# Graph message layer on one core: three changes ahead of the periods (first receivers, x's differences, inverse lengths)

## The reference

```
r = edge_vec / norm(edge_vec);  sh1 = sqrt(3) * r
xs, xd = x[src], x[dst]                       # sender's and receiver's rows
w  = relu(emb @ w1 / sqrt(10)) @ w2 / sqrt(16)    # per-edge weights, 512 and 384 of them
s_t, v_t  = products of (xs, xd) with w and sh1   # first layer
scal, gates, vecs = products of (s_t, v_t) with w2 and sh1
edge_out = [tanh(scal), vecs * tanh(gates)] * edge_weight
out = layernorm(x + segment_sum(edge_out, dst))
```

## Time and profile before

| | us |
|---|---|
| median of 3 runs | 6613.86 |
| these runs | 6610.04 to 6614.21 |
| profiled execution, its own time | 6605.81 |
| span of that execution | 6604.0 |
| first DMA of the first period's loads issued at | 62.45 |
| first product of the periods on VectorE (L1233) starts at | 105.46 |

### The profile page before, as it was taken

How to read it: one execution, slowest core, us unless ns; L and a number is a source line. 1 busy time by engine, 2 the same in 40 slices (tenths; PEclk the granted TensorE clock), 3 DMA queues, 4 the chain that set the end, 5 groups by cost and what they waited for, 6 DMA issues and landing times.

```text
span 6604.0 us, 217789 instructions
## 1 busy us (share of the span) xinstructions
PE 5916.6 (90%) x67802; PEld 5648.0 (86%) x67802; DVE 5987.5 (91%) x7727; ACT 4058.7 (61%) x12100; POOL 5021.9 (76%) x6871
## 2 busy tenths in 40 slices
PE   2999999999999999999999999999989999999997
PEld 2888888888888888888888888888888888888887
DVE  6999999999999999999999999999999999999998
ACT  3666666666666666666666666666666666666664
POOL 4777777777777777777777777777777777777774
PEclk9999999999999999999999999999999999999998
DMA  4444444444444444444444444444444444444442
GB/s 126 86 89 84 86 87 85 85 87 86 84 86 88 84 87 86 84 86 88 84 86 88 84 86 88 84 88 86 86 89 84 86 88 84 88 86 86 87 85 54
DMA packets 1671528, 569.93 MB, mean 86 GB/s; under 512 B 1535556, under 2 KB 1619493, under 8 KB 1670946
## 3 DMA queue, kind: packets, MB, share of 16 engines
q1 hardware_dynamic: 1568321, 516.43, 35.3%
q0 software_dynamic: 103168, 53.03, 6.0%
HBM read 302.19 MB, written 7.26 MB: 47 GB/s over the span
## 4 chain that ended last, share of the span: by engine, by line
PE 75%; issue 13%; DVE 5%; ACT 3%; another core or an unknown queue 3%; DVEq 1%; ACTq 0%; DMA 0%; POOL 0%; SPq 0%; POOLq 0%
PE p L982 42%; PE pw L977 18%; PE p L1068 4%; PE ph L965 2%; PE ph L954 2%; PE p L1061 2%; PE p L1063 1%; PE p L1029 1%; PE p L1011 1%; DVE prods L1275 1%; ACT hot_t L741 1%; PE p L1012 1%; DVEq L1434 1%; ACT osum L820 0%
## 5 line engine op out<-in xcount | busy, mean ns | idle before, releaser
L982 PE MATMUL p<-identity,prods 128*128 128x128 f32 x29016 | 3642.6, 279 | 7.8 <-issue 6.7
L647 POOL DMA_INDIRECT nodes<-x_rows,idx x3224 | 3114.5, 966 | 603.7 <-issue 515.9
L982 PEld LDWEIGHTS p<-identity,prods 128*128 128x128 f32 x29016 | 3292.0, 146 | 36.5 <-issue 12.3
L977 PE MATMUL pw<-w_stack,hid_t 128*128 128x128 bf16 x22568 | 1702.4, 223 | 116.2 <-issue 52.4
L977 PEld LDWEIGHTS pw<-w_stack,hid_t 128*128 128x128 bf16 x22568 | 1433.6, 100 | 216.7 <-issue 98.2
L1275 DVE TENSOR_TENSOR prods<-pw,M 128x1024 f32<-128x1024 f32 x806 | 977.1, 1212 | 38.5 <-PE pw L977 24.8
L1233 DVE TENSOR_TENSOR prods<-pw,V 128x2048 f32<-128x2048 f32 x403 | 914.4, 2269 | 9.4 <-ACT acc L926 6.3
L1252 DVE TENSOR_TENSOR prods<-pw,S 128x1024 f32<-128x1024 f32 x403 | 491.8, 1220 | 327.6 <-remote 190.7
L838 ACT ACTIVATE off_hot<-node_iota,off_base 128x42 f32<-128x42 f32 x3216 | 752.6, 317 | 13.0
L1285 DVE TENSOR_TENSOR prods<-pw,VT 128x1536 f32<-128x1536 f32 x403 | 705.2, 1750 | 23.9 <-PE pw L977 19.4
L594 POOL TENSOR_TENSOR msg<-th,late 128x128 f32<-128x128 f32 x403 | 164.0, 407 | 728.7 <-ACT th L819 390.8
(11 more groups left out here) (130 smaller groups left out, 8205.5 us busy)
## 6 DMA issues: line engine op xcount, KB each, us to landing
dstb<-in_dst SPq DMA_DIRECT2D x403, 504.0 KB
nodes<-x_rows,idx POOLq DMA_INDIRECT x3224
emb_stack<-emb_parts SPq DMA_DIRECT2D x2418, 20.0 KB
emb<-in_emb_t SPq DMA_DIRECT2D x403, 40.0 KB
hid_t<-hid_parts SPq DMA_TRANSPOSE x806
idx<-in_src SPq DMA_DIRECT2D x403, 4.0 KB
xw<-x SPq DMA_DIRECT2D x403, 7.9 KB
vecs<-in_vec SPq DMA_DIRECT2D x403, 12.0 KB
```

Of the source, the lines that this page charges most:

```text
L647: nc.gpsimd.indirect_dma_start(nodes[:, p, t, side, :], None, x_rows, bass.IndirectOffsetOnAxis(ap=idx[:, p, side, t:t + 1], axis=0)).then ...
L977: mm = nc.tensor.matmul(pw[:, slot, t, :], hid_t[:, layer, a.par, t, :], w2_stack[:, lo:lo + W], start=True, stop=True)
L982: return nc.tensor.matmul(out, column, identity[:, :], start=first, stop=last, is_transpose=True)
```

## The change

Three things, all ahead of the periods. `base_i` is no longer loaded. TensorE waits for `s_excess` and turns the four columns of `span[:, 2, :]` into one row with four small matmuls, into `p1`; VectorE copies the row (and the last super's number) into `base_i`. The four subtractions of x's pieces go from VectorE to GpSimd, in its list between `emb_less_second` of super 0 and `partition_all_reduce`, for which it now also waits until all eight steps of `x_cast` are done; `x_parted` is gone. Squares, sums, roots and reciprocals of the lengths are made in three parts each (1088, 1088 and 1056 of 3232 per partition), and roots and reciprocals move from the body of i = -1 to ahead of the program: ScalarE's roots ahead of its reading of the flag, VectorE's reciprocals behind its own.

```
@@ SyncE
-            sp.dma_start(base_i[0:1, 0:FULL], dst[0:FULL * SUPER].rearrange("(a s e) -> a s e", a=1, e=SUPER)[:, :, 0],
-                         allow_slow_non_contiguous=True).then_inc(s_base_in, 16)
-            if NS != FULL:
-                sp.dma_start(base_i[0:1, FULL:NS], dst[E - SUPER:E - SUPER + 1].rearrange("(a s) -> a s", a=1)
-                             ).then_inc(s_base_in, 16)
...
-                sp.wait_ge(s_inv, 1)
+                sp.wait_ge(s_inv, len(thirds))
...
-            sp.wait_ge(x_parted, 1)
+            sp.wait_ge(x_cast, 8)
             sp.dma_start(x3.rearrange("(p b) a f -> p (b a f)", p=P),
@@ GpSimd
             emb_less_second(At(0, 0))
+            for h in range(2):
+                half = xn[:, h * (NB // 2):(h + 1) * (NB // 2), :]
+                parts = x_parts[:, h * (NB // 2):(h + 1) * (NB // 2), :, :]
+                pool.wait_ge(x_cast, 4 * h + 1)
+                nc.gpsimd.tensor_tensor(x_rest, half, parts[:, :, 0, :], ALU.subtract).then_inc(x_cast, 1)
+                pool.wait_ge(x_cast, 4 * h + 3)
+                nc.gpsimd.tensor_tensor(parts[:, :, 2, :], x_rest, parts[:, :, 1, :], ALU.subtract).then_inc(x_cast, 1)
+            pool.wait_ge(x_cast, 8)
             pool.wait_ge(s_excess, 1)
             nc.gpsimd.partition_all_reduce(excess_all[:, :], excess_one[:, :], P, RMAX).then_inc(s_excess_all, 1)
@@ ScalarE
                 act.wait_ge(x_in, 16 * len(x_pieces))
+                wait(act, x_cast, 4 * h)
                 nc.scalar.activation(parts[:, :, 0, :], half, ACT.Copy).then_inc(x_cast, 1)
...
-            nc.scalar.activation(all_vectors, all_vectors, ACT.Square).then_inc(s_squared, 1)
+            for lo, hi in thirds:
+                nc.scalar.activation(all_vectors[:, 3 * lo:3 * hi], all_vectors[:, 3 * lo:3 * hi], ACT.Square
+                                     ).then_inc(s_squared, 1)
+            for g, (lo, hi) in enumerate(thirds):
+                act.wait_ge(s_norm2, g + 1)
+                nc.scalar.activation(inv[:, lo:hi], inv[:, lo:hi], ACT.Sqrt).then_inc(s_length, 1)
             act.wait_ge(row_node_done, 2)
             act.wait_ge(s_general, 1)
...
-                    if i == -1:
-                        act.wait_ge(s_norm2, 1)
-                        nc.scalar.activation(inv[:, :], inv[:, :], ACT.Sqrt).then_inc(s_length, 1)
@@ TensorE
             pe.wait_ge(s_const, 11)
+            pe.wait_ge(s_excess, 1)
+            for c in range(SCAN):
+                mm = nc.tensor.matmul(p1[0:1, P * c:P * c + P], span[:, 2, c:c + 1], identity[:, :], start=True, stop=True)
+            mm.then_inc(s_bases, 1)
             pe.wait_ge(s_general, 1)
@@ VectorE
-            for h in range(2):
...
-                nc.vector.tensor_tensor(x_rest, half, parts[:, :, 0, :], ALU.subtract).then_inc(x_cast, 1)
...
-            dve.sem_inc(x_parted, 1)
...
+            dve.wait_ge(s_bases, 1)
+            nc.vector.tensor_copy(base_i[0:1, 0:FULL], p1[0:1, 0:FULL]).then_inc(s_base_in, 1)
+            if NS != FULL:
+                nc.vector.tensor_copy(base_i[0:1, FULL:NS], span[0:1, 2, SCAN:SCAN + 1]).then_inc(s_base_in, 1)
...
-            dve.wait_ge(s_base_in, 32 if NS != FULL else 16)
+            dve.wait_ge(s_base_in, NS - FULL + 1)
             flag = nc.vector.value_load(general[0:1, 0:1], min_val=0, max_val=1)
...
-            dve.wait_ge(s_squared, 1)
-            nc.vector.tensor_reduce(inv[:, :], all_vectors.rearrange("p (e k) -> p e k", k=3), AX.X, ALU.add
-                                    ).then_inc(s_norm2, 1)
+            for g, (lo, hi) in enumerate(thirds):
+                dve.wait_ge(s_squared, g + 1)
+                nc.vector.tensor_reduce(inv[:, lo:hi], all_vectors[:, 3 * lo:3 * hi].rearrange("p (e k) -> p e k", k=3), AX.X,
+                                        ALU.add).then_inc(s_norm2, 1)
+            for g, (lo, hi) in enumerate(thirds):
+                dve.wait_ge(s_length, g + 1)
+                nc.vector.reciprocal(inv[:, lo:hi], inv[:, lo:hi]).then_inc(s_inv, 1)
...
-                    if i == -1:
-                        dve.wait_ge(s_length, 1)
-                        nc.vector.reciprocal(inv[:, :], inv[:, :]).then_inc(s_inv, 1)
```

More of the change, by code:

```diff
@@ L220, in build_gnn_layer @@
         s_base_in = sem("s_base_in")
+        s_bases = sem("s_bases")
         s_scan_in = sem("s_scan_in")
@@ L223, in build_gnn_layer @@
         x_cast = sem("x_cast")
-        x_parted = sem("x_parted")
         x3_out = sem("x3_out")
@@ L390, in build_gnn_layer @@
         vec_pieces = in_pieces(all_vectors, vec.rearrange("e k -> (e k)"), vec_rows_full, 3 * ER, 0, 3 * ER, 3 * vec_last)
+        third_of = 16 * -(-ER // 48)
+        thirds = [(g * third_of, min(ER, (g + 1) * third_of)) for g in range(3)]
         per_bank = 512 // F
@@ L511, in _ @@
             sp.wait_ge(x3_out, 16)
-            sp.wait_ge(s_base_in, 32 if NS != FULL else 16)
+            sp.wait_ge(s_base_in, NS - FULL + 1)
             sp.wait_ge(s_general, 1)
@@ L923, in body @@
                     if i in (0, 1):
-                        act.wait_ge(s_norm2, 1)
+                        act.wait_ge(s_norm2, 3)
                         lo, hi = (0, ACC // 2) if i == 0 else (ACC // 2, ACC)
@@ L1195, in _ @@
             nc.vector.tensor_reduce(excess_one[:, :], excess[:, :], AX.X, ALU.max).then_inc(s_excess, 1)
-            for h in range(2):
-                half = xn[:, h * (NB // 2):(h + 1) * (NB // 2), :]
-                parts = x_parts[:, h * (NB // 2):(h + 1) * (NB // 2), :, :]
-                dve.wait_ge(x_cast, 4 * h + 1)
-                nc.vector.tensor_tensor(x_rest, half, parts[:, :, 0, :], ALU.subtract).then_inc(x_cast, 1)
-                dve.wait_ge(x_cast, 4 * h + 3)
-                ins = nc.vector.tensor_tensor(parts[:, :, 2, :], x_rest, parts[:, :, 1, :], ALU.subtract)
-                ins.then_inc(x_cast, 1)
-                dve.wait_ge(x_cast, 4 * h + 4)
-            dve.sem_inc(x_parted, 1)
             dve.wait_ge(s_const, 11)
```

## The result

The changed kernel takes 6663.95 us in the median (6654.34 to 6666.22, four runs), the kernel before beside it 6614.03 (6610.04 to 6622.14, four runs): ratio 1.0071, interval 1.0054 to 1.0089. It is 50 us slower where 14.6 us faster was forecast, and the prediction is wrong. The profiled execution has a span of 6664.3 us, 60.3 over that of before.

The account below looks back on a forecast made before the run. With TensorE 90% busy, only the start of the periods was taken to move. Gains of 11.3 us (GpSimd and ScalarE path) and 3.3 us (inverse lengths) made 14.6, so 6613.86 became 6599.3 us, range 6593 to 6610.

Parts of the forecast that it names:

- What bounds the kernel: Whole span: TensorE is busy 90% and a period's work is untouched, so only the start of the periods can move.
- The last sentence of the prediction: Signs of a wrong forecast: all-reduce over 3 us off 47, x3 later than 45, or a period's work changing pace.
- Part 1: Start, SyncE: without base_i's loads x3 is stored at 42, lands at 49.1, and SyncE reaches the first period 12.4 us earlier.
- Part 2: Start, GpSimd: four subtractions at 3.2 us each, from 19.91 to 37.6, so x3's store at 42 does not wait.
- Part 3: Start, behind GpSimd's subtractions: reload 7.7, all-reduce 1.8, sums from 48.3, row_shift at 59.8; gain cut to 11.3 us.
- Part 4: Start, inverse lengths in thirds: their store at 90.2 no longer waits 4.06 us for VectorE; less 0.8, gain 3.3 us.
- The sum: Whole kernel: 11.3 + 3.3 = 14.6 us gained, all at the start, giving 6599.3 us.
- A: Start, SyncE: x_rows's backlog holds whatever stands next, x3 goes at 54.4, only 3.3 us gained, 6610.6; chance 0.12.
- B: Start, GpSimd's path longer: 3.8 to 4.5 us a subtraction or reload over 10, 6601.5 to 6606; chance 0.2.
- C: Start, GpSimd's path shorter (2.6 to 3.0 us, reload 6), SyncE's path decides, gain 12.4 + 3.3 to 4.1, 6597.5; chance 0.17.
- D: Start, GpSimd: subtractions cost 16.5 ns a column, 26 us each, so 77 us lost, 6690; chance 0.03.

Follow-up runs that it names:

- f2: Changed kernel plus two idle semaphore increments on SyncE in place of the two base_i loads, against the kernel before: 6542.06 us beside 6555.18, ratio 0.9979.
- j2: The same kernel as f2, run again against the kernel before: 6543.88 us beside 6553.51, ratio 0.9986.
- h3: f2's kernel plus 32 increments at the start of VectorE's list, against the kernel before: 6023.02 us beside 6037.13, ratio 0.9975.
- e1: Kernel before with only the base_i loads replaced by TensorE's matmuls and VectorE's copies, against the kernel before: 6087.09 us beside 6039.16, ratio 1.0075.
- h1: Kernel before plus 63 idle increments on SyncE ahead of the loop, against the kernel before: 6098.14 us beside 6037.13, ratio 1.0101.
- h2: Kernel before plus 62 idle increments on SyncE ahead of the loop, against the kernel before: 6094.9 us beside 6037.13, ratio 1.0099.
- h4: Kernel before plus four increments on SyncE inside the loop, once per pair of periods, against the kernel before: 6115.19 us beside 6037.13, ratio 1.0132.

## Why the prediction was wrong, step by step

- **What bounds the kernel**: this step failed. "So it can only move the point at which the periods begin to run at their pace" was drawn from TensorE's 90%. SyncE is not in that row, and its waits over the periods were not read. With two instructions fewer ahead of its loop, SyncE takes 0.22 us longer around the back branch of every pair, at an edge of its list. At the higher clock it has no slack (no row of waits), and the pair is 0.31 us longer, 197 times; on the chip of the result it has 7%, and the pair is 0.36 us longer all the same. So the periods lost 73 us where the prediction had nothing, and the start's 13.2 stand against them. That the edit would touch SyncE's pace could not be read from the trace of before; that SyncE has little to spare could. The last sentence of the prediction named this case, and gave it no chance.
- **Part 1**: right. The stacks went out and the last ones were held, to 40.02; x3 at 40.06 for 42. But it landed 10.9 us later and not 7.1, at 50.99 for 49.1. So idx was 10.5 us earlier, not 12.4: this term is 1.9 too large. The copy to x_rows landed only at 43.0 (issued at 12.18, 30.8 us), so x3's store ran beside it for its first 3 us, where before x3 went out 10 us after that landing (44.3). That this made the store longer was not tried.
- **Part 2**: right. 3.15 us for 3.2, the last ending at 37.64 for 37.6. The Trainium skill's scaled 3.44 lies above the row.
- **Part 3**: the order was right, two sizes were off. The reload was 6.12 us for 7.7 (the Trainium skill's 6 is the nearer), and the all-reduce 0.38 for 1.80. So the sums began at 45.45 for 48.3, and row_shift stood at 56.84 for 59.8, directly behind the last root. (The squares began at 39.36, when the vectors had landed, and not at 34.4; the first of them was done before VectorE had read the flag, so it cost nothing.) ScalarE's emb_first was done at 62.28, and its path ceased to set the end. GpSimd's subtraction came at 65.78 for 65.25, by the other path: its third gather, which hangs on SyncE's idx, ended at 58.29, and the reload behind it took 7.48 us. That is 1.6 behind the 64.15 of that path, and 10.8 us earlier for 11.3. That it comes so near is luck: a term 1.9 too large and a path that was too long met.
- **Part 4**: the store went at 90.80 for 90.2, and the wait for the reciprocal was gone. Behind the transpose it took 7.97 us and not 5.32, so 2.65 went where 0.8 was set, inside the bounds of 0 and 3.
- **The sum** of 14.6 for the start is 13.2 in the trace of after. With the place restored the whole kernel gains 13.1 us in f2 and 9.6 in j2, and 14.1 in h3, which also moves VectorE's list. So with the place restored the gain is 0.14 to 0.25%, where some 0.2% was forecast.
- **Rivals**: A fell (x3 at 40). B fell, C's mechanism was the one that ran, without its larger gain. D fell: 3.15 us. None of them had a period in it. The rival on the slower side was sought in the edited lines only. By their own terms B's times are 6601.3 to 6605.3, and C's reach from 6597.4 to 6598.2; the slips are under 1 us.

## What to carry to other kernels

Before an edit ahead of a loop is called harmless, look at every queue's waits in the loop, SyncE's too. An engine without waits there passes on what it is given (e1, h1, h2 and h4), and here one with 7% of waits did so as well. Where such a loop is short, find where it lies in its engine's list. If the pace changes by a fixed step for each pass though no line of the loop was edited, compare the step behind the back branch in both traces, and shift the list by a few idle instructions before judging the edit. Time an edit at a start with and without that shift.

## What the hardware showed that I had not expected

- Edges in SyncE's list, three of them, 128 instructions apart (behind 79, 207 and 335): 128 to 146 ns at the branch, 65 to 95 ns where a loop runs over one, some 400 ns at the first crossing in straight code, at places that don't depend on the instruction.
- A VectorE operation on 128x5 took 1.79 us and its neighbours 0.17. It ran from 31.10 to 32.89, and GpSimd's subtraction, begun at 29.73, ended at 29.73 + 3.15 = 32.88. In the trace of before the same holds the other way: the all-reduce took 1.80 us beside VectorE's subtraction of 1.78, and takes 0.38 alone. The Trainium skill, "SBUF — State Buffer", section "SBUF: two separate sides", calls the port pair of the two engines an exclusive lock in which the loser blocks for a whole instruction; both traces agree.
- The hold of SyncE moved on to the next DMAs with many small pieces: 13.97 us for six emb stacks, until 40.02, where base_i's load was held until 41.02.
